# Images innermost in the DRAM buffers of a recurrent scan, fewer and larger transfers, and VectorE instead of TensorE for an addition

## The chip, the cores and the metric

The kernel runs on one core of a Trainium2 chip. The metric is the device time of one execution in microseconds. Its engines here are TensorE (PE, with its weight loads as PEld), VectorE (DVE), ScalarE (ACT), GpSimd (POOL) and SyncE (SP), which only issues DMA transfers; a queue of an engine is written SPq or ACTq.

## The reference

x has 4 images, 512 channels and 64 x 64 pixels, so 4096 tokens an image, all in float32. Four layers follow each other, each of the form x + layer(group norm of x). Layers 1 and 3 are Fourier mixers, layer 2 a gate; they are not touched. Layer 0 is a recurrent layer over the tokens with 8 heads of 64 and chunks of 16 tokens:

```python
def step(carry, inp):
    W1c, b1c = carry
    xq, xk, xv, et = inp
    Z1 = xk @ W1c + b1c
    grad = _ln_l2_bwd(Z1, xv - xk, g, bb)
    Attn1 = jnp.tril(xq @ xk.swapaxes(-1, -2))
    b1_bar = b1c - jnp.tril(et) @ grad
    Z1_bar = xq @ W1c - et * Attn1 @ grad + b1_bar
    last_eta = et[..., -1, :, None]
    W1n = W1c - (last_eta * xk).swapaxes(-1, -2) @ grad
    b1n = b1c - (last_eta * grad).sum(-2, keepdims=True)
    return ((W1n, b1n), xq + _ln(Z1_bar, g, bb, EPS_IN))
...
return _ln(out, post_w, post_b, EPS_IN) @ o_w.T
```

The result, with the bias that `post_b` gives and with x added, is x1, the input of layer 1.

## The kernel before

Layer 0 has two parts. `project` makes, for every block of 512 tokens of an image, keys, targets and rates (a record of 196 numbers a token and head, tensor `records` in DRAM) and the rotated queries (`queries`). ScalarE issues both stores (L1203, L1205), one pair for each 128 tokens. At its end ScalarE writes rows of zeros behind the records of every image, which the scan's loads ahead of need may touch (L1234, 8 transfers).

`scan_and_read` then runs 256 steps of 16 tokens, over all 4 images and 8 heads at once, in two groups of two images (g = 0 and 1). The partitions are 4 head pairs x 16 tokens x 2 heads of a pair. A step of a group goes: TensorE makes Z from the state and the keys (`project_k`, L2107 and L2113), ScalarE sums its squares (`spread`, L1798), VectorE makes the gradient from it (`gradients`, L1963 to L1989), GpSimd the sum of gradients and the scaled gradient (`stored`), TensorE adds to the state in PSUM (`update`, L2125) and ScalarE copies the state out (`state_out`, L1791). The state of the next step needs this one, so each group is a chain.

Beside the chain runs the reading of 128 tokens of one image, a tile. There are 32 blocks (`sc`) of 128 tokens (eight steps) and 4 images, so 128 tiles, one for every two steps; two steps with one tile are called a slot here. A tile is worked on with a lag: `KQ`, `OUT`, `NORM`, `PROJ`, `LEAVE` = 4 to 8 slots behind the scan. The even or the odd step of a slot (`at.odd`) has its fixed part of it. `project` of the tile is L2195: 4 x 4 products with the output weights, and for each of the 4 channel blocks one product of the identity with the image (L2198), which adds x in PSUM. `leave` (ScalarE, L1845) adds the bias while it copies out; `moments` (VectorE, L1997) takes the statistics for the next layer.

All engines run a program written out by hand: eight steps twice in the body of a loop (`Fori(1, SC // 2)`), the first and last turns outside it. Instructions of an engine run in that order, so a wait holds all behind it. SyncE issues every transfer of the scan from one queue, and waits in it for what a transfer needs:

```python
for g in range(GR):
    sp.wait_ge(state_ps[g].sem, state_ps[g].at(s, -1))
    load_record(g, (c + 2) % RING, s + 2)      # two transfers
...
for g in range(GR):
    sp.wait_ge(stored_sb[g].sem, stored_sb[g].at(s, 1))
    # two stores into gradients
```

Then in an even step the tile's gradients and sums are loaded (`grad_sb`, `b_sb`), in an odd one the query of the next tile, once GpSimd has read the one before (`qb_sb`), and the keys of a later block (`k_in`, which TensorE turns, L2095). y is stored and x loaded a tile at a time in odd steps. `queries` are turned by TensorE in L2176, the result of a tile in L2159.

## Time and profile before

| | |
|---|---|
| median of 3 runs (lowest, highest) | 6241.13 us (6234.36, 6241.5) |
| profiled execution, its own time | 6242.9 us |
| its span, first to last instruction | 6241.0 us |
| busy over the span: PE, VectorE, ScalarE, GpSimd | 86%, 63%, 38%, 38% |
| projection, about | 215 to 1645 us |
| scan, about | 1719 to 4340 us |
| Fourier layers and gate | the rest |
| DMA packets | 823279, of them 357224 under 512 bytes |

Busy time is the time in which an engine has an instruction running; the rest is waiting. An engine's share is a mean over parts with different limits, so it is read for each part. A line such as L2113 is that line of the kernel. "issue" as the cause of a wait means that nothing in the profile shows what the engine waited for.

### The profile page before, as it was taken

Reading aid. Unit: us, or ns where it says so; the run is one execution under the profiler, and the core shown is the slowest. Engines: PE = TensorE matmul, PEld = TensorE weight load, DVE = VectorE, ACT = ScalarE, POOL = GpSimd, SP = SyncE. Lnnn points to the kernel's source line nnn. Section 1 sums busy time; section 2 is a strip of 40 time slices with the busy share of each in tenths; the row PEclk is TensorE's granted clock in tenths of the full one; section 3 lists DMA queues with packets and bytes.
Section 4 is the critical chain, followed back from the end, with each engine's and each line's share of the span. In section 5 each row is a group of like instructions: output and inputs, shape, how many; then the busy total and the mean of one; then the engine's idle time right before and its main releaser. Section 6 shows DMA issues by size and latency. Waiting matters only on the chain. (4 is left out here: it accounts for less than half of the span.)

```text
span 6241.0 us, 144090 instructions
## 1 busy us (share of the span) xinstructions
PE 5393.6 (86%) x42556; PEld 3821.0 (61%) x42556; DVE 3919.7 (63%) x14026; ACT 2368.3 (38%) x6675; POOL 2385.5 (38%) x3910
## 2 busy tenths in 40 slices
PE   1799999999588888888888888888799999599999
PEld 0344444444267777777777777777666666377777
DVE  5566666666377777777767777777566666544444
ACT  0111111111055555555555555555333333233333
POOL 0244444444255455555545554454122222122222
PEclk9899999999779899989999998999899999799999
DMA  6233333333344444444444444444212221222221
GB/s 246 72 128 120 127 120 127 120 128 120 127 106 119 125 119 123 118 122 118 119 119 121 120 120 120 118 122 126 98 77 87 87 87 45 78 88 87 87 87 70
DMA packets 823279, 693.73 MB, mean 111 GB/s; under 512 B 357224, under 2 KB 758000, under 8 KB 811664
## 3 DMA queue, kind: packets, MB, share of 16 engines
q1 hardware_dynamic: 732304, 542.54, 29.1%
q10 hardware_dynamic: 90240, 142.75, 6.1%
q8 instruction: 294, 4.82, 0.3%
q14 instruction: 441, 3.61, 0.2%
HBM read 402.96 MB, written 282.20 MB: 110 GB/s over the span
## 5 line engine op out<-in xcount | busy, mean ns | idle before, releaser
L1390 PE MATMUL proj_ps<-proj_w_sb,proj_h 128*128 128x512 f32 x3072 | 1345.6, 596 | 0.0
L1390 PEld LDWEIGHTS proj_ps<-proj_w_sb,proj_h 128*128 128x128 f32 x3072 | 577.2, 190 | 743.4 <-issue 716.6
L2195 PE MATMUL scan_ps_y<-scan_o_t,proj_wo_sb 128*128 128x128 f32 x4096 | 648.2, 307 | 2.1 <-ACT scan_o_t L1827 2.1
L1312 DVE SCALAR_TENSOR_TENSOR proj_lin<-proj_ps,proj_rstd,proj_wbias_sb 128x512 f32<-128x512 f32 x384 | 284.5, 748 | 545.8 <-PE proj_ps L1390 544.8
L2195 PEld LDWEIGHTS scan_ps_y<-scan_o_t,proj_wo_sb 128*128 128x128 f32 x4096 | 565.1, 214 | 50.8 <-issue 8.6
L1737 POOL TENSOR_TENSOR scan_b_step<-scan_core,scan_rate_last 128x128 f32<-128x128 f32 x512 | 318.6, 622 | 650.5 <-DVE scan_core L1984 650.5
L1963 DVE TENSOR_TENSOR scan_zg<-scan_ps_z,scan_gain 128x128 f32<-128x128 f32 x512 | 146.1, 285 | 563.1 <-ACT scan_square L1798 518.0
L1798 ACT ACTIVATE scan_square<-scan_ps_z 128x64 f32<-128x64 f32 x1024 | 218.6, 220 | 651.0 <-PE scan_ps_z L2113 645.4
L1791 ACT COPY scan_state_w<-scan_ps_w 128x512 f32<-128x512 f32 x480 | 281.3, 586 | 476.1 <-PE scan_ps_w L2125 455.5
L2125 PE MATMUL scan_ps_w<-scan_step,scan_record 64*128 64x128 f32 x4088 | 386.5, 312 | 12.4 <-DVE scan_step L1989 11.9
L1266 POOL TENSOR_TENSOR proj_gk<-proj_rec,proj_gain_sb 128x256 f32<-128x256 f32 x256 | 181.5, 729 | 554.5 <-DVE proj_rec L1333 554.5
L1260 POOL TENSOR_TENSOR proj_by_cos<-proj_lin,proj_rope 128x512 f32<-128x512 f32 x256 | 340.7, 1341 | 137.5 <-DVE proj_lin L1312 108.0
L266 POOL TENSOR_TENSOR fourier_spec<-fourier_prod 128x448 f32<-128x448 f32 (+1 forms) x80 | 86.7, 1084 | 696.3 <-DVE fourier_prod L410 696.3
L281 ACT COPY fourier_turned<-fourier_psT 128x512 f32<-128x512 f32 (+3 forms) x289 | 156.7, 550 | 476.0 <-PE fourier_psT L480 476.0
L2125 PEld LDWEIGHTS scan_ps_w<-scan_step,scan_record 64*128 64x128 f32 x4088 | 301.7, 208 | 49.8 <-DVE scan_step L1989 18.2
L1729 POOL TENSOR_TENSOR scan_rate<-scan_rstd,scan_record 128x2 f32<-128x2 f32 x512 | 102.8, 201 | 598.0 <-DVE scan_rstd L1966 593.2
L1744 POOL TENSOR_TENSOR scan_b_sum<-scan_b_step,scan_b_sum 128x128 f32<-128x128 f32 x512 | 309.6, 605 | 44.9 <-POOL scan_b_step L1737 7.1
L706 POOL TENSOR_TENSOR fourier_spec<-fourier_prod 128x448 f32<-128x448 f32 (+1 forms) x80 | 86.5, 1082 | 619.8 <-DVE fourier_prod L799 619.8
L487 PEld LDWEIGHTS fourier_psD<-fourier_mats,fourier_turned 128*128 128x128 f32 x2148 | 270.4, 192 | 78.8 <-ACT fourier_turned L281 35.2
L487 PE MATMUL fourier_psD<-fourier_mats,fourier_turned 128*128 128x128 f32 x2148 | 288.5, 277 | 34.4 <-DVE fourier_spec L389 31.8
L2113 PE MATMUL scan_ps_z<-scan_state_w,scan_k_t 128*32 128x64 f32 x7680 | 207.2, 228 | 108.0 <-ACT scan_state_w L1791 107.2
L831 PEld LDWEIGHTS fourier_psD<-fourier_mats,fourier_turned 128*128 128x128 f32 x2080 | 260.5, 191 | 43.7 <-issue 22.3
(290 smaller groups left out, 12327.7 us busy)
## 6 DMA issues: line engine op xcount, KB each, us to landing
scan_record<-records SPq DMA_DIRECT2D x1032, 98.0 KB
records<-proj_rec ACTq DMA_DIRECT2D x128, 784.0 KB, 3.6
scan_k_in<-records SPq DMA_DIRECT2D x266, 128.0 KB
spectra<-fourier_spec SPq DMA_DIRECT2D x16, 2112.0 KB, 6.4
fourier_spec<-spectra SPq DMA_DIRECT2D x16, 2112.0 KB, 8.2
stats_x<-x SPq DMA_DIRECT2D x16, 2048.0 KB, 7.7
proj_h<-x SPq DMA_DIRECT2D x32, 1024.0 KB, 7.1
queries<-proj_q ACTq DMA_DIRECT2D x128, 256.0 KB, 3.7
```

Of the source, the lines that this page charges most:

```text
L487: done = pe.matmul(psD[t % 2][:, col:col + P], turned[t % 2][:, j * P:(j + 1) * P], mat, start=True, stop=True)
L831: done = pe.matmul(psD[q][:, col:col + P], turned[q][:, j * P:(j + 1) * P], mat, start=n == 0, stop=n == len(terms) - 1)
L1260: g_.tensor_tensor(by_cos[q][:, n].rearrange("p (a e) -> p a e", e=32), lin[q][:, n].rearrange("p (a e) -> p a e", e=32), cos, ALU.mult).t ...
L1312: v.scalar_tensor_tensor(lin[q][:, n], ps[q][n][:], rstd[k][:, j:j + 1], T.wbias[:, n], ALU.mult, ALU.add).then_inc(lin_sb.sem, 1)
L1390: last = pe.matmul(ps[j % 2][n][:], h[k][:, ct, j * P:(j + 1) * P], T.w[:, n, ct], start=ct == 0, stop=ct == CT - 1)
L1737: v.tensor_tensor(b_step[g][:], core[g][:], rate_last[g][:, :, 2:3].broadcast_to([P, PB, HD]), ALU.mult).then_inc(b_step_sb[g].sem, 1)
L1744: v.tensor_tensor(b_sum[g][(c + 1) % RING][:], b_step[g][:], b_sum[g][c % RING][:], ALU.add).then_inc(b_sum_sb[g].sem, 1)
L1791: a.copy(state_of(g, at)[:].rearrange("p r b a e -> p r (b a e)"), ps_w[:, :, g].rearrange("p r b a e -> p r (b a e)")).then_inc(state_sb[ ...
L1798: a.activation(square[:, g, b], ps_z[g][:, b * HD:(b + 1) * HD], ACT.Square, accum_out=ssq[g][:, b:b + 1]).then_inc(ssq_sb[g].sem, 1)
L2113: done = pe.matmul(ps_z[g][32 * a:32 * a + 32, b * HD:(b + 1) * HD], k_t[q][PB * g + b][:, a, CS * at.c:CS * at.c + CS].rearrange("p t n - ...
L2125: done = pe.matmul(ps_w[:, r, g, b].rearrange("p a e -> p (a e)"), record[g][at.ring][rows, b, 0:2 * HD], step[g][rows, b].rearrange("p a ...
L2195: pe.matmul(ps_y[:, n], T.wo[:, ct, n * P:(n + 1) * P], o_t[:, ct], start=ct == 0, stop=False)
```

## The change

The DRAM buffers `records`, `gradients` and `sum_snapshots` get another order of dimensions, with the images inside the tokens. A record load then takes all four images at once; a gradient store takes the two images of a group, a snapshot too. Records are written by two transfers for each 128 tokens, one for each head of the pairs; a tile's gradients are read by two. Queries, x and y move for four tiles at once, with buffers four times as large, two of each. `leave` goes from ScalarE to VectorE and adds bias and image in one instruction of three operands; the identity products go. The rows of zeros are written at the start of the projection. Buffers that only the projection needs are released before the scan.

```diff
-    rec = dram("records", (B, NH // 2, TOK + 2 * P, 2, RW))
+    rec = dram("records", (NH // 2, TOK + 2 * P, 2, B, RW))
-    grad = dram("gradients", (B, NH // 2, TOK, 2, HD))
-    s_snap = dram("sum_snapshots", (TOK // P * B * P, HD))
+    grad = dram("gradients", (NH // 2, TOK, 2, B, HD))
+    s_snap = dram("sum_snapshots", (TOK // P, 2, P, B // 2, HD))
...
-                    act.dma_start(rec[bass.ds(b, 1), :, bass.ds(g * 512 + j * P, P)].rearrange("o a t n e -> (o t) a (n e)"),
-                                  rec_sb[:, j].rearrange("p (a n) e -> p a (n e)", n=2)).then_inc(rec_out[j].sem, 16)
+                    for n in range(2):
+                        act.dma_start(rec[:, bass.ds(g * 512 + j * P, P), n, bass.ds(b, 1)].rearrange("a t o e -> (o t) a e"),
+                                      rec_sb[:, j].rearrange("p (a n) e -> p a n e", n=2)[:, :, n]).then_inc(rec_out[j].sem, 16)
...
             normalise(0, 0, 0)
+
+            act.wait_ge(init.sem, init.at(0, 1))
+            for a in range(NH // 2):
+                for n in range(2):
+                    act.dma_start(rec[a, TOK + n * P:TOK + (n + 1) * P].rearrange("t n b e -> t (n b e)"), zero[:]).then_inc(pad_out.sem, 16)
             rows_out(0)
...
-        x_sb = [sb(f"x_in{q}", [P, CT, P]) for q in range(2)]
-        y_sb = [sb(f"y{q}", [P, CT, P]) for q in range(2)]
+        x_sb = [sb(f"x_in{q}", [P, UNITS, P]) for q in range(2)]
+        y_sb = [sb(f"y{q}", [P, UNITS, P]) for q in range(2)]
...
-            def load_record(g, ring, s):
-                for b in range(PB):
-                    sp.dma_start(record[g][ring][:, b, :], rec[PB * g + b, :, bass.ds(s * CS, CS)].rearrange("a t n e -> a (t n) e")
-                                 ).then_inc(rec_in[g][ring].sem, 16)
+            def load_record(ring, s):
+                sp.dma_start(record[ring][:].rearrange("p b e -> p (b e)"), rec[:, bass.ds(s * CS, CS)].rearrange("a t n b e -> a (t n) (b e)")
+                             ).then_inc(rec_in[ring].sem, 16)
...
-                        load_record(g, (c + 2) % RING, s + 2)
...
+                    load_record((c + 2) % RING, s + 2)
+                if c == 1 and (scan or p == 0) and (not isinstance(v, int) or v * 2 + p):
+
+                    sp.dma_start(x_sb[1 - p][:], x_view[:, :, bass.ds((v * 2 + p - 1) * P, P)]).then_inc(x_loaded[1 - p].sem, 16)
                 if scan:
                     for g in range(GR):
                         sp.wait_ge(stored_sb[g].sem, stored_sb[g].at(s, 1))
-                        for b in range(PB):
-                            sp.dma_start(grad[PB * g + b, :, bass.ds(s * CS, CS)].rearrange("a t n e -> a (t n) e"),
-                                         stored[g][c % 2][:, b, :]).then_inc(grad_gone[g][c % 2].sem, 16)
+                        sp.dma_start(grad[:, bass.ds(s * CS, CS), :, PB * g:PB * g + PB].rearrange("a t n b e -> a (t n) b e"),
+                                     stored[g][c % 2][:]).then_inc(grad_gone[g][c % 2].sem, 16)
+                if c == 7 and (not isinstance(v, int) or v):
+
+                    sp.wait_ge(y_done.sem, y_done.at(v * 8 + p * 4 - 4, 0))
+                    sp.dma_start(o_view[:, :, bass.ds((v * 2 + p - 2) * P, P)], y_sb[p][:]).then_inc(y_gone[p].sem, 16)
...
+                elif scan:
+                    if c == 3:
+
+                        if not isinstance(v, int):
+                            sp.wait_ge(qb_sb.sem, qb_sb.at(v * 8 + p * 4 - 4, 0))
+                        sp.dma_start(q_sb[p][:].rearrange("p b h e -> p b (h e)"), q_in[:, bass.ds((v * 2 + p) * P, P)].rearrange("b n c -> n b c")
+                                     ).then_inc(q_loaded[p].sem, 16)
...
-                for n in range(CT):
-                    done = a.activation(y_sb[q][:, n], ps_y[:, n], ACT.Identity, bias=T.wo_bias[:, n:n + 1])
-                done.then_inc(y_done.sem, 1)
...
+            def leave(tile):
+                t, b, sc, par, half = tile
+                q = b % 2
+                dve.wait_ge(y_ps.sem, y_ps.at(t, 1))
+                dve.wait_ge(x_loaded[par].sem, x_loaded[par].at(half, 16))
+                dve.wait_ge(y_gone[par].sem, y_gone[par].at(half, 0))
+                dve.wait_ge(stats_sb.sem, stats_sb.at(t, 0))
+                for n in range(CT):
+                    done = v.scalar_tensor_tensor(y_sb[par][:, b * CT + n], ps_y[:, n], T.wo_bias[:, n:n + 1], x_sb[par][:, b * CT + n], ALU.add, ALU.add)
+                done.then_inc(y_done.sem, 1)
...
-                elif norm:
-                    head_norms(norm)
+                else:
+                    if norm:
+                        head_norms(norm)
+                    if gone:
+                        leave(gone)
...
-                    pe.matmul(ps_y[:, n], T.wo[:, ct, n * P:(n + 1) * P], o_t[:, ct], start=ct == 0, stop=False)
-                if n == 0:
-                    pe.wait_ge(x_loaded[b % 2].sem, x_loaded[b % 2].at(sc * 2 + b // 2, 16))
-                done = pe.matmul(ps_y[:, n], T.ident[:], x_sb[b % 2][:, n], start=False, stop=True)
+                    done = pe.matmul(ps_y[:, n], T.wo[:, ct, n * P:(n + 1) * P], o_t[:, ct], start=ct == 0, stop=ct == CT - 1)
```

## Rows read from the trace of the kernel before

**Rows 1.** Order in time of PE: start us, length us, what [wait before it <- releaser].
```profile
1718.62 0.66 PE L2113 MATMUL scan_ps_z<-scan_state_snap,scan_k_t 128*32 128x64 f32 x16 [1.35 <-ACT scan_state_snap L1791]
...
2703.18 0.65 PE L2159 MATMUL scan_ps_turn<-proj_ident_sb,scan_on 128*128 128x128 f32 x4 [0.38 <-ACT scan_on L1821]
...
2720.35 0.65 PE L2159 MATMUL scan_ps_turn<-proj_ident_sb,scan_on 128*128 128x128 f32 x4 [0.37 <-ACT scan_on L1821]
...
2727.65 0.66 PE L2176 MATMUL scan_ps_turn<-proj_ident_sb,scan_q_in 128*128 128x128 f32 x4 [2.17 <-DMA scan_q_in<-queries]
...
4334.98 0.41 PE L2113 MATMUL scan_ps_z<-scan_state_w,scan_k_t 128*32 128x64 f32 x16
```

**Rows 2.** Groups by line, 2500 to 3000 us: count | busy us, mean ns | idle before.
```profile
L1971 DVE SCALAR_TENSOR_TENSOR scan_t_row<-scan_zg,scan_rstd,scan_record 128x64 f32<-128x64 f32 x194 | 46.1, 278 | 0.0
...
L2198 PE MATMUL scan_ps_y<-scan_x_in,proj_ident_sb 128*128 128x128 f32 x192 | 40.0, 293 | 0.0
```

**Rows 3.** Busy us by window: length, PE, PEld, DVE, ACT, POOL, clock, DMA, GB/s.
```profile
2500.00:3000.00 500.00, 425.33 (x5597) 372.12 (x5595) 362.21 (x1830) 281.74 (x974) 255.88 (x530) 0.91 0.45 120
```

**Rows 4.** Waits, 2500 to 3000 us: total us, times, longest us.
```profile
DVE scan_zg L1963 <- ACT scan_square L1798: 95.4, 44, 7.0
...
PE scan_ps_turn L2176 <- DMA scan_q_in<-queries: 37.8, 18, 4.8
...
DVE scan_zg L1963 <- issue: 12.6, 3, 4.9
```

**Rows 5.** Order in time of SyncE's queue, one slot: start us, length us.
```profile
2720.29 4.10 SPq L1677 DMA_DIRECT2D gradients<-scan_stored  x4
2724.64 0.48 SPq L1633 DMA_DIRECT2D scan_q_in<-queries  x1
...
2726.97 2.94 SPq L1623 DMA_DIRECT2D scan_record<-records  x4
2730.11 2.96 SPq L1677 DMA_DIRECT2D gradients<-scan_stored  x4
...
2738.32 0.42 SPq L1667 DMA_DIRECT2D x<-scan_y  x1
```

**Rows 6.** DMA queues in 2729:2733, 2733.5:2734.5, 2735:2736, 1650:1664: packets, MB, share of 16.
```profile
q1 hardware_dynamic: 435, 0.33, 26.2%
...
q1 hardware_dynamic: 282, 0.07, 31.7%
...
q1 hardware_dynamic: 623, 0.27, 97.5%
...
q10 hardware_dynamic: 3424, 5.19, 104.1%
```

**Rows 7.** Order in time of VectorE, parts of three slots.
```profile
2679.68 0.29 DVE L1963 TENSOR_TENSOR scan_zg<-scan_ps_z,scan_gain 128x128 f32<-128x128 f32 x1 [4.93 <-issue]
...
2700.93 0.28 DVE L1963 TENSOR_TENSOR scan_zg<-scan_ps_z,scan_gain 128x128 f32<-128x128 f32 x1
...
2708.92 0.29 DVE L1963 TENSOR_TENSOR scan_zg<-scan_ps_z,scan_gain 128x128 f32<-128x128 f32 x1 [0.79 <-ACT scan_square L1798]
...
2718.46 0.28 DVE L1963 TENSOR_TENSOR scan_zg<-scan_ps_z,scan_gain 128x128 f32<-128x128 f32 x1
```

**Rows 8.** The page's groups by line, the projection's additions.
```profile
L1312 DVE SCALAR_TENSOR_TENSOR proj_lin<-proj_ps,proj_rstd,proj_wbias_sb 128x512 f32<-128x512 f32 x384 | 284.5, 748 | 545.8 <-PE proj_ps L1390 544.8
```

**Rows 9.** Order in time between projection and scan.
```profile
1645.50 11.70 ACTq L1234 DMA_DIRECT2D records<-proj_zero  x8
...
1671.80 0.34 SPq L1615 DMA_DIRECT2D scan_gain<-gain_rows  x1
```

**Rows 10.** Busy by window, columns as in rows 3.
```profile
1646.00:1666.00 20.00, 0.00 (x0) 0.00 (x0) 0.00 (x0) 0.00 (x0) 0.00 (x0) 0.50 1.02 364
1666.00:1672.00 6.00, 0.00 (x0) 0.00 (x0) 0.00 (x0) 0.00 (x0) 0.00 (x0) 0.50 0.00 1
```

**Rows 11.** The page's DMA issues: count, KB each, median us to landing.
```profile
queries<-proj_q ACTq DMA_DIRECT2D x128, 256.0 KB, 3.7
```

More of the change, by code:

```diff
@@ L1432, in each @@
             return [sb(f"{n}{g}", shape) for g in range(GR)]
-        record = many("record", [P, PB, RW], RING)
+        record = [sb(f"record{q}", [P, B, RW]) for q in range(RING)]
         stored = many("stored", [P, PB, HD], 2)
@@ L1541, in scan_and_read @@
         q_loaded = [one(f"q_loaded{q}", 16) for q in range(2)]
-        grad_in = [one(f"grad_loaded{q}", 48) for q in range(2)]
+        grad_in = [one(f"grad_loaded{q}", 64) for q in range(2)]
         x_loaded = [one(f"x_loaded{q}", 16) for q in range(2)]
@@ L1750, in gained @@
             def gained(tile):
-                t, b, sc, _ = tile
+                t, b, sc, par, half = tile
                 pool.wait_ge(zo_sb.sem, zo_sb.at(t, 2))
@@ L1817, in normed @@
             def normed(tile):
-                t, b, sc, _ = tile
+                t, b, sc, par, half = tile
                 act.wait_ge(oshift_sb.sem, oshift_sb.at(t, 1))
@@ L1823, in outputs_turned @@
             def outputs_turned(tile):
-                t, b, sc, _ = tile
+                t, b, sc, par, half = tile
                 act.wait_ge(turn_o.sem, turn_o.at(t, 1))
@@ L1829, in outputs_out @@
             def outputs_out(tile):
-                t, b, sc, _ = tile
+                t, b, sc, par, half = tile
                 act.wait_ge(zgain_sb.sem, zgain_sb.at(t, 0))
@@ L1854, in query_turned @@
             def query_turned(tile):
-                t, b, sc, _ = tile
+                t, b, sc, par, half = tile
                 act.wait_ge(turn_q.sem, turn_q.at(t, 1))
@@ L1860, in head_roots @@
             def head_roots(tile):
-                t, b, sc, _ = tile
+                t, b, sc, par, half = tile
                 act.wait_ge(hsq_sb.sem, hsq_sb.at(t, 1))
@@ L1866, in output_squares @@
             def output_squares(tile):
-                t, b, sc, _ = tile
+                t, b, sc, par, half = tile
                 act.wait_ge(o_done.sem, o_done.at(t, 1))
@@ L1872, in output_root @@
             def output_root(tile):
-                t, b, sc, _ = tile
+                t, b, sc, par, half = tile
                 act.wait_ge(ovar_sb.sem, ovar_sb.at(t, 2))
@@ L1878, in body @@
             def body(at, scan):
-                kq, out, norm, proj, gone = (at.tile(n) for n in (KQ, OUT, NORM, PROJ, LEAVE))
+                kq, out, norm, proj = (at.tile(n) for n in (KQ, OUT, NORM, PROJ))
                 following = Place(at.v, at.p, at.c + 1) if at.c < 7 else Place(at.v + at.p, 1 - at.p, 0)
@@ L2011, in head_sums @@
             def head_sums(tile):
-                t, b, sc, _ = tile
+                t, b, sc, par, half = tile
                 dve.wait_ge(zsq_sb.sem, zsq_sb.at(t, 1))
@@ L2017, in variance @@
             def variance(tile):
-                t, b, sc, _ = tile
+                t, b, sc, par, half = tile
                 dve.wait_ge(nmean_sb.sem, nmean_sb.at(t, 1))
@@ L2026, in shift_of @@
             def shift_of(tile):
-                t, b, sc, _ = tile
+                t, b, sc, par, half = tile
                 dve.wait_ge(ostd_sb.sem, ostd_sb.at(t, 1))
@@ L2034, in head_norms @@
             def head_norms(tile):
-                t, b, sc, _ = tile
+                t, b, sc, par, half = tile
                 dve.wait_ge(hstd_sb.sem, hstd_sb.at(t, 1))
@@ L2044, in weights @@
             def weights(tile):
-                t, b, sc, _ = tile
+                t, b, sc, par, half = tile
                 dve.wait_ge(kq_ps.sem, kq_ps.at(t, 1))
@@ L2146, in tile_weighted @@
             def tile_weighted(tile):
-                t, b, sc, par = tile
+                t, b, sc, par, half = tile
                 for n in range(2):
@@ L2154, in tile_outputs_turn @@
             def tile_outputs_turn(tile):
-                t, b, sc, par = tile
+                t, b, sc, par, half = tile
                 pe.wait_ge(on_sb.sem, on_sb.at(t, 1))
@@ L2189, in tile_project @@
             def tile_project(tile, n):
-                t, b, sc, par = tile
+                t, b, sc, par, half = tile
                 if n == 0:
```

160 lines of the change are left out of this document (63 added, 97 removed).

## Prediction

> **What bounds the kernel now.** I read the page first, for the stages, then windows of each stage, and in the scan the waits, SyncE's queue, the DMA packets and VectorE's order in time. The projection before it runs with PE busy all the time, and the Fourier layers behind it are not touched, so the change must earn its time in the scan, from the first product of L2113 at 1718.6 us to the last at 4335.0 [rows 1] and some 5 us of its own tail: 2621 us for 256 steps, or 128 slots of two steps and one tile, 20.5 us a slot. In a stretch of 500 us with 24 slots (192 records of the identity product, eight a slot [rows 2]), PE is busy 85% at a mean granted clock of 0.91, VectorE 72% [rows 3]. Neither is full, yet two runs of L2159, one a slot, can stand 17.2 us apart [rows 1]: that is what the engines need when nothing is late. What is late is the query tile: PE waits for it in 18 of 24 slots, 37.8 us in total [rows 4], for instance 2.17 us at 2727.65 [rows 1], and with PE stand ScalarE's squares and VectorE, which waits 95.4 us for them [rows 4].
>
> Why is it late? SyncE's queue shows the sum [rows 5]: per slot eight record loads (2.94 us for four, twice), eight gradient stores (4.10 and 2.96 us for four), and some eight more of 0.4 to 0.5 us each. That is 5.9 + 7.1 + 3.6 = 16.6 us, and with the gaps between them about 18.5: the queue issues back to back. The query load stands behind four stores in it, and may only be issued when the tile before is read (one buffer per parity).
>
> Under the queue lies a second limit. While only record packets of 784 bytes move, 435 packets take 26.2% of 16 engines for 4 us [rows 6], about four engines: 435 / 4 = 109 per engine, 36.8 ns each. The stores of 256 bytes show 31.7%, with two packets of an engine overlapping; on four engines they take 4 / 282 us = 14.2 ns each. Where 512-byte packets of other transfers move, the share is 97.5%, so those use all 16, 16 / 623 us = 25.7 ns each. The Trainium skill has a rule for this (DMA: Bandwidth & Descriptors, "Why a DMA increments its semaphore by 16 and not by 1"): the slowest dimension of both sides decides how many engines take part. The trace agrees, for both kinds of transfer have the four head pairs outermost on the DRAM side. The four engines' need per slot: records 8 x 32 packets x 36.8 ns = 9.4 us; stores 8 x 32 x 14.2 = 3.6; 1536 packets of 512 bytes over 16, 2.5; keys and sums 1.0; queries 0.7. Sum 17.2 us of 20.5.
>
> **The change, part by part.**
> *SyncE's queue.* Per slot remain 2 record loads, 4 stores, 2 gradient, 2 sum and 2 key loads, and per four slots 2 snapshots and one x, y and query transfer. At 0.74 us for each of the first six (4.10 / 4 = 1.03 for stores at worst) and 0.5 for 7.25 others: 4.4 + 3.6 = 8.0 us, 9.2 at worst. It is no longer a limit. Transfers of 1 MB have no row from this queue; their issue costs between the 0.4 us of a quarter of the size and four times that, 1.6 us, with 11 us of free queue per slot over them.
> *Queries, x, y.* The query for four tiles is issued at step 3 of eight and first read six steps later, two buffers deep. The stall of 37.8 / 24 = 1.6 us a slot goes, and with it PE's slow clock behind it. x is loaded seven steps ahead; y is stored at step 7 with nine steps until its buffer is wanted. Price zero, covered by these steps; without cover a 1 MB transfer of 512-byte packets takes 128 x 25.7 ns = 3.3 us.
> *Records.* One load of 128 x 3136 bytes in place of four. The DRAM side keeps the form of the packets that moved on four engines in the row (four head pairs outermost), so I count four again: 32 packets each. A packet of 1568 bytes takes 16 x 1.041 x 14 us / 3424 = 68 ns [rows 6], 23 bytes per ns, against 21 for 784. At the better rate 136 ns, 4.4 us per step in place of 4.7; at the worse 147 ns, no gain. I take 4.4.
> *Stores and gradient loads.* Half the stores, 512 bytes if batch and head elements merge, the same bytes on the same four engines: 3.6 us a slot at 14.2 ns per 256 bytes (3.3 at 25.7 per 512). The gradient load is two of 512 x 256 bytes: 64 x 14.2 = 0.9 in place of 0.8. The four engines' need becomes 8.7 + 3.6 + 1.7 + 0.9 + 1.0 + 0.7 = 16.6 us a slot.
> *PE.* Four identity products a slot go, eight records, 40.0 / 24 = 1.67 us busy [rows 2], of which part overlaps the neighbours; 1.2 to 1.7 us off a need of at most 17.2 leaves about 15.9.
> *VectorE.* It gets the four additions (`leave`), after `head_norms` and before the second gradient of the even step. In the stretch it waits 95.4 + 12.6 us [rows 4], so its own need, with gaps from write to read, is (500 - 108) / 24 = 16.3 us a slot. The fast slot agrees: from 2700.93 to 2718.46 are 17.53 us with one wait of 0.79 [rows 7], 16.7 at most. The new instruction has the form of L1312 at 128 columns. L1312 takes 748 ns for 512 columns [rows 8] and L1971 278 for 64 [rows 2], by a straight line 345 ns for 128; as they overlap, I take 0.27 us from start to start. Both ends: 4 x 0.22 = 0.9 and 4 x 0.34 = 1.4; I take 1.1 with the wait. VectorE's need becomes 17.4 us, the largest of the four (queue 8 to 9, four DMA engines 16.6, PE 15.9). The 0.79 us that VectorE waited for PE in the fast slot is filled by the additions, so it is not added.
> *ScalarE* loses four activations; it waits 0.6 us for PE and more in a slot, so this is nothing.
> *Turns of the loop.* Every eighth slot has a stall of VectorE that no engine releases: 3 in the stretch, 12.6 us [rows 4], one of 4.93 [rows 7]. It stays, 16 x 4 = 64 us.
> *Remainder.* Slots after a turn run PE at the slow clock, the snapshot adds a copy, and large transfers hit the records now and then. No row prices these together; between 0 and 1 us a slot, I take 0.3, 38 us.
> Scan after: 128 x 17.4 + 64 + 38 = 2329 us, 292 less.
> *The zero rows* of the records are written at the start of the projection. Now their eight DMAs begin at 1645.50 behind the last product, and the scan's first transfer is issued at 1671.80 [rows 9]. The DMA engines are idle from 1666, 6 us before that [rows 10]. The last store before them, issued just ahead of 1645.5, lands in 3.7 us [rows 11], at 1649; with the same 6 us the scan begins at 1655: 17 us saved. At the start of the projection 6.4 MB at the rate of now, 5.19 MB in 14 us [rows 6], take 17 us beside the first products; ScalarE issues them where `rows_out(0)` waits for GpSimd anyway. If the queue pushes back as it does now (11.70 us for eight [rows 9]), PE starts up to 6 us late. With a quarter of the packets I take 0. Two stores for one per row block: 0.4 us of an idle ScalarE.
> *Tail.* The last y is 1 MB, 2 to 3 us more; the last tiles lose PE work of 1.2 us each: -3 together.
> Sum: -292 - 17 - 3 = -312 us from the profiled execution's 6242.9 us, which gives 5931; the median of the runs is 1.8 us lower, so 5930.
>
> **Rivals.**
> A. *VectorE is the new bound*, as above: 5930, with 5870 to 6010 for additions of 0.9 to 1.4 us and a remainder of 0 to 0.7.
> B. *The four DMA engines stay the bound.* For it: 16.6 us against 17.4 is close, records may gain nothing, and before the change a need of 17.2 came with 20.5, because bursts meet. The 1 MB transfers make bursts larger. Against: no record was ever waited for, and loads run two steps ahead. If half of the present surplus of 3.3 us stays on 17.4, a slot takes 19.0: 128 x 19.0 + 64 = 2496, -125 - 20: 6098. By the rule of the Trainium skill (DMA: Bandwidth & Descriptors, "Why a DMA increments its semaphore by 16 and not by 1") merging transfers doesn't cure the four engines, since the outermost dimension is still four; the 4.4 us a step taken above counts with that.
> C. *More than I count.* If the turn of the loop and the remainder shrink with the DMA waits (fewer instructions to fetch), 128 x 17.2 + 20: -400 and -20: 5820.
> D. *Slower: PE's clock.* VectorE as the bound leaves PE idle 1.5 to 2.5 us a slot in pieces. If the granted clock sits at its lower level (1.2 GHz) instead of 2.4 for much of the slot, PE's 15.9 us grow to 15.9 x (1 + f); the slot passes 20.5 at f = 0.3, and with f = 0.6 is 25.4: +630 us, 6850. For it: the mean is 0.91 even now [rows 3]. Against: the fast slot had gaps of under 1 us and kept the clock; what lowered it were stalls of 2 us and more, and these go.
> E. *No change:* the queue was a symptom and the second gradient's chain holds the slot. The 17.2 us slots speak against it. 6241.
>
> **How the numbers follow.** A 0.62, B 0.20, C 0.10, D 0.05, E 0.03. The likeliest gives 5930. The range runs from between A and C, 5850, to B, 6110, and leaves out most of C, the far end of B, D and E. Under 0.2% (12 us) a measurement of this kernel tells nothing. Faster 0.92, same 0.03, slower 0.05.
>
> **What would show it.** SyncE's queue with gaps of 8 us and more a slot; no wait of L2176 for a DMA; slots of L2159 at 17.4 to 18, with VectorE's waits under 2 us a slot; `leave` at 0.25 to 0.34 us each; the scan starting 17 us earlier. It is wrong if record or gradient loads appear in the waits (B), if the granted clock of the scan falls under 0.8 (D), or if VectorE waits for the squares in every slot, a chain that I held to be covered.

## The result, and the profile after

The changed kernel takes 6131.8 us (median of 4 runs, 6119.6 to 6136.6) against 6241.3 for the kernel before beside it: a ratio of 0.9824, 95% interval 0.9807 to 0.9841, 109 us less. The forecast was 5930 us, in a range of 5850 to 6110. The direction is right; about a third of the gain came. The profiled execution took 6136.6 us, with a span of 6134.8.

PE's order in time gives the scan's first and last state product, as in [rows 1]:

```profile
1700.38 0.66 PE L2103 MATMUL scan_ps_z<-scan_state_snap,scan_k_t 128*32 128x64 f32 x16 [1.35 <-ACT scan_state_snap L1780]
...
4234.01 0.41 PE L2103 MATMUL scan_ps_z<-scan_state_w,scan_k_t 128*32 128x64 f32 x16
```

The scan starts 18.2 us earlier, as the 17 us of the zero rows had it (zeros_last below tests the reason). But it still lasts 2533.6 us where it lasted 2616.4, 19.8 us a slot in place of 20.4; the forecast, turns and remainder included, was 2329 / 128 = 18.2. So nearly all that is missing is missing inside the scan. The busy time by window (columns as in [rows 3]) says that no engine filled up:

```profile
2500.00:3000.00 500.00, 426.46 (x5554) 369.19 (x5553) 402.83 (x1988) 266.31 (x897) 264.71 (x546) 0.89 0.50 123
```

VectorE, the announced bound, is busy 81% of the time, PE 85% as before, at a granted clock of 0.89 in place of 0.91. Its additions are there, 100 of them in the 500 us, so 25 slots. One lasts 342 ns; as they overlap, they keep VectorE busy for 28.0 / 25 = 1.1 us a slot, the price forecast:

```profile
L1976 DVE SCALAR_TENSOR_TENSOR scan_y<-scan_ps_y,proj_wo_bias_sb,scan_x_in 128x128 f32<-128x128 f32 x100 | 28.0, 342 | 0.0
```

What ended the idle time is in the waits of the whole scan, 1700 to 4235 us (total, times, longest):

```profile
DVE scan_zg L1939 <- ACT scan_square L1787: 266.2, 121, 16.5
...
PE scan_ps_out L2129 <- DMA scan_b_in<-sum_snapshots: 116.4, 59, 4.8
...
POOL scan_rate L1718 <- DMA scan_record<-records: 60.8, 49, 3.9
...
DVE scan_t_row L1947 <- DMA scan_record<-records: 39.4, 40, 3.5
...
PE scan_ps_turn L2085 <- DMA scan_k_in<-records: 20.0, 18, 2.5
...
POOL scan_stored L1736 <- DMA gradients<-scan_stored: 10.2, 14, 1.3
```

The first row is not new: over its scan (1718 to 4336 us) the kernel before had 514.0 us of this wait. The query's wait [rows 4] is gone, and in its place stand waits for the sums, the records, the keys and the stores. The prediction had named this: "It is wrong if record or gradient loads appear in the waits (B)". And SyncE's queue, which was to have gaps of 8 us and more a slot, is occupied for 17.5 of 19.8 us (waits between the transfers of a row included), with fewer but longer issues (compare [rows 5]):

```profile
2560.69 3.38 SPq L1683 DMA_DIRECT2D scan_b_in<-sum_snapshots  x2
2564.39 0.62 SPq L1624 DMA_DIRECT2D scan_record<-records  x1
2565.20 0.39 SPq L1658 DMA_DIRECT2D scan_x_in<-x  x1
2565.81 8.93 SPq L1662 DMA_DIRECT2D gradients<-scan_stored  x2
2574.99 1.65 SPq L1629 DMA_DIRECT2D scan_k_in<-records  x2
```

The record issue shown is cheap (0.62 us for what took 2.9). Two gradient stores behind a record and a 1 MB image load take 8.93 us to issue, 8.1 of them the first store alone, and two sum loads 3.38. With the records on more engines (rec_by_pair, below) two sum loads are issued in 0.89.

Last, the number of engines. In 2522 to 2523 us only record packets move, 3136 bytes each (packets, MB, share of 16 engines):

```profile
q1 hardware_dynamic: 32, 0.10, 25.8%
```

A quarter of 16 engines, four, 129 ns a packet, 4.1 us a load: a little better than the 136 ns and 4.4 us forecast. By the prediction's own sum, with this rate, the four engines would need some 16 us of a slot. The slot takes 19.8. The sum takes every packet at the length that it has when its kind moves alone, and among other traffic packets are longer: over 1800 to 3900 us a record packet lasted 172 ns on the mean. If an engine carries one at a time, a slot's two loads take 2 x 32 x 0.172 = 11.0 us of the four engines and not 8.3, an estimate from these two figures.

### The profile page after: what moved, and what is told of

Read it like the earlier page. It is cut to its first block and busy times, and to the rows that moved or that the text cites. A ratio compares the mean times of both kernels' runs of the same rounds, so it can differ in the third digit from the quotient of the medians.

```text
span 6134.8 us, 138259 instructions
## 1 busy us (share of the span) xinstructions
PE 5355.8 (87%) x41532; PEld 3773.6 (62%) x41532; DVE 4049.2 (66%) x14538; ACT 2249.2 (37%) x6163; POOL 2386.6 (39%) x3910
## 5 line engine op out<-in xcount | busy, mean ns | idle before, releaser
L2185 PE MATMUL scan_ps_y<-scan_o_t,proj_wo_sb 128*128 128x128 f32 x4096 | 624.4, 300 | 1.6 <-DVE scan_y L1976 0.9
L2185 PEld LDWEIGHTS scan_ps_y<-scan_o_t,proj_wo_sb 128*128 128x128 f32 x4096 | 544.2, 207 | 48.8 <-issue 5.5
L2140 PE MATMUL scan_ps_out<-scan_grad_in,scan_weigh 128*128 128x64 f32 x2048 | 337.2, 334 | 0.0
L2140 PEld LDWEIGHTS scan_ps_out<-scan_grad_in,scan_weigh 128*128 128x128 f32 x2048 | 317.2, 244 | 20.2 <-issue 10.8
L487 PEld LDWEIGHTS fourier_psD<-fourier_mats,fourier_turned 128*128 128x128 f32 x2148 | 271.2, 193 | 81.6 <-issue 38.3
L1947 DVE SCALAR_TENSOR_TENSOR scan_t_row<-scan_zg,scan_rstd,scan_record 128x64 f32<-128x64 f32 x1024 | 272.1, 306 | 39.7 <-DMA scan_record<-records 39.4
```

The lines of the kernel that those rows point to most:

```text
L487: done = pe.matmul(psD[t % 2][:, col:col + P], turned[t % 2][:, j * P:(j + 1) * P], mat, start=True, stop=True)
L1947: v.scalar_tensor_tensor(t_row[g][:, b], zg[g][:, b], rstd[g][:, b:b + 1], record[at.ring][:, PB * g + b, 2 * HD:3 * HD], ALU.mult, ALU.ad ...
L2140: done = pe.matmul(ps_out[n][:, a, 0:HD], weigh[n][:, a], grad_sb[b % 2][:, 2 * a + n], start=False, stop=True, skip_group_check=True)
L2185: done = pe.matmul(ps_y[:, n], T.wo[:, ct, n * P:(n + 1) * P], o_t[:, ct], start=ct == 0, stop=ct == CT - 1)
```

## The experiments

Four theories. *1:* the four DMA engines that carry records and stores remain the bound, and the long issues are its symptom (rival B). *1a:* the 1 MB transfers add to it, by more than their bytes. *2:* VectorE is the bound (the prediction). *3:* SyncE's queue by its number of issues. The expectations of the first runs call 1a theory 2. The kernel before took 6240.5, 6249.5, 6253.7 and 6246.0 us beside the four groups of runs, so kernels are compared by their ratio to it. All intervals are about 0.0016 to either side. Percentages from here on are differences of these ratios, so shares of the time before.

| kernel | edit | median us | ratio to before |
|---|---|---|---|
| after | the change | 6131.8 | 0.9824 |
| rec_by_pair | record load in 4 transfers, by head pair | 5840.7 | 0.9362 |
| rec_by_image | in 4 transfers, by image | 6019.1 | 0.9651 |
| rec_by_group | in 2 transfers, of two images | 6003.0 | 0.9599 |
| rec_padded | 1 transfer, 784-byte pieces | 6174.1 | 0.9877 |
| leave_back | additions back on ScalarE and PE | 6128.6 | 0.9822 |
| rec_by_pair_leave_back | rec_by_pair and leave_back together | 5811.9 | 0.9296 |
| all_by_pair | the same, and the stores by head pair | 5825.4 | 0.9313 |
| all_by_pair_by_tile | all_by_pair, and images, outputs, queries by tile | 5847.3 | 0.9349 |
| by_tile | after, images, outputs, queries by tile | 6068.4 | 0.9709 |
| by_tile_by_group | by_tile and rec_by_group | 5961.0 | 0.9538 |
| by_tile_leave_back | by_tile and leave_back: the layout alone | 6074.4 | 0.9725 |
| x_first | after, image load ahead of the record load | 6066.4 | 0.9711 |
| zeros_last | after, zero rows at the projection's end | 6150.3 | 0.9836 |
| before_queries | before, queries four tiles at a time | 6220.4 | 0.9970 |
| before_rec_by_pair | before, record load by head pair | 5887.4 | 0.9414 |

**Which engines carry the records: rec_by_pair.**

```diff
-sp.dma_start(record[ring][:]..., rec[:, bass.ds(s * CS, CS)].rearrange("a t n b e -> a (t n) (b e)"))
+for a in range(HP):
+    sp.dma_start(record[ring][32 * a:32 * a + 32]..., rec[a, bass.ds(s * CS, CS)].rearrange("t n b e -> (t n) (b e)"))
```

> The changed kernel, with each step's record load issued as four transfers of one head pair each (32 partitions of 3136 B) in place of one transfer whose outermost dimension is the 4 head pairs. Theory 1 (four DMA engines are the bound): in the trace of the changed kernel, stretches with nothing but records under way show 25.8% of the engines' time, four engines of sixteen, and a load alone takes 4 x 32 packets of 0.125 us over 4 engines, 4.0 us a step or 8.0 us of the 19.8 us slot, mixed with other traffic more. Spread over sixteen engines it needs a quarter of that: SyncE's issues of sums, keys and gradients fall from 2.6 to 5.3 us back to 0.9 to 1.4 us, VectorE's waits for the record (39.4 us) and PE's for the sums (117.4 us) go, and a slot falls towards its fast ones, 16.7 us: 64 x 2 x (19.8 - 17.0) = 360 us less at best, so 5770 to 5900 us. Theory 2 (the 1 MB transfers of images, outputs and queries hold up everything behind them): record loads are as late as before, 6100 to 6150 us. Theory 3 (the issuing of SyncE's queue is the bound): six more issues a slot at 0.5 to 0.7 us add 3 to 4 us to a queue that holds 19.8 us already, 6200 us or more.

Measured 0.9362: 4.6% below the changed kernel, as theory 1 had it. Theory 3 is out, since SyncE issues six transfers a slot more. VectorE did not set the slot of the changed kernel either, since its work is the same here and the slot is shorter. Not all of the 4.6% is owed to the engines: four transfers that stay on the four engines give 1.7% (rec_by_image, below), so the engines' own part, at the same number of issues, is 2.9%. Its busy row for 2500 to 3000 us, and its first and last state product:

```profile
2500.00:3000.00 500.00, 443.01 (x6337) 383.70 (x6338) 454.84 (x2262) 304.65 (x1024) 298.23 (x621) 0.98 0.55 142
```

```profile
1703.69 0.55 PE L2104 MATMUL scan_ps_z<-scan_state_snap,scan_k_t 128*32 128x64 f32 x12 [1.35 <-ACT scan_state_snap L1781]
...
3934.68 0.41 PE L2104 MATMUL scan_ps_z<-scan_state_w,scan_k_t 128*32 128x64 f32 x16
```

A slot takes 17.4 us, PE's granted clock is back at 0.98, and in this stretch no compute engine waits for a DMA: VectorE's wait for the squares is 3.1 us where it was 40.5. By the page, a quarter of a record lands 2.2 us after its issue; two sum loads are issued in 0.89 us:

```profile
scan_record<-records SPq DMA_DIRECT2D x1032, 98.0 KB, 2.2
```

```profile
2523.74 0.89 SPq L1684 DMA_DIRECT2D scan_b_in<-sum_snapshots  x2
```

And in 2516.5 to 2517 us, where 33 of 49 packets are records, the DMA engines show

```profile
q1 hardware_dynamic: 49, 0.10, 76.1%
```

twelve engines' worth in place of four, and 33 record packets started in half a microsecond where 32 took a whole one. The rule of the Trainium skill (DMA: Bandwidth & Descriptors, "Why a DMA increments its semaphore by 16 and not by 1"), that the slowest dimensions of the two sides set the number of engines, fits: that dimension was 4 before the edit, with 25.8% of 16 engines in the trace, and is 32 after it, with 76.1%.

**The same on the kernel before: before_rec_by_pair.**

```diff
-for b in range(PB):
-    sp.dma_start(record[g][ring][:, b, :], rec[PB * g + b, :, bass.ds(s * CS, CS)].rearrange("a t n e -> a (t n) e"))
+for a in range(HP):
+    sp.dma_start(record[ring][32 * a:32 * a + 32], rec[:, a, bass.ds(s * CS, CS)].rearrange("b t n e -> (t n) b e"))
```

> The kernel before, its DRAM layout, sums, stores, queries and images as they were, with only the record tile joined to one for all images and loaded by four transfers of one head pair (32 partitions of 4 pieces of 784 B) in place of four of one image (128 pieces, head pairs outermost): as many issues as before. If the four DMA engines bound the kernel before too, they lose half of their load (8.7 of 17.2 us a slot), the query wait (37.8 us of 500) and the holds of SyncE go, and slots fall from 20.5 to 17.5 to 19 us, 5880 to 6050 us, and the change's larger and fewer transfers were not what the kernel lacked. If SyncE's issues bound it (the prediction's first reading: 16.6 to 18.5 us of issues a slot), as many issues leave it at 6180 to 6240 us.

Measured 0.9414, 5887 us, at the low end of what the four engines were to give. With the old layout, 784-byte pieces, as many issues as before and nothing batched, the way in which one load is cut gives 5.9%, over three times what the whole change gives. This is the cleanest of the experiments: pieces and issues are the same in number and size, and what differs is which pieces a transfer holds (and that a load waits for both groups of images). What the whole change adds to it is 0.5% (0.9362 for rec_by_pair). In 2500 to 3000 us PE's granted clock is 0.99, and the query's wait has shrunk from 37.8 to 8.0 us by itself:

```profile
PE scan_ps_turn L2175 <- DMA scan_q_in<-queries: 8.0, 4, 2.5
```

Both limits that the prediction saw in the kernel before (SyncE's queue, the late query) were symptoms of the four engines that it put under them.

**The query's wait alone: before_queries.** The kernel before with `q_sb` for four tiles and one 1 MB load at the fourth step, eight slots ahead.

```diff
-load_query(t, b, sc)
+sp.dma_start(q_sb[at.p][:]..., q_in[:, bass.ds((v * 2 + at.p) * P, P)].rearrange("b n c -> n b c"))
```

> The kernel before, with one part of the change alone: the queries of four tiles are loaded by one transfer of 1 MB, eight slots ahead, in place of one of 256 KB a tile that PE waited for (37.8 us of 500 us, 18 waits). If that wait was a cause of its own, its removal gives 37.8 / 500 x 2561 = 190 us, 6050 us. If it was only where a full set of four DMA engines showed (records and stores need 17.2 us a slot of them), the wait moves to the record, the sums or the stores, and the gain is under 60 us: 6180 to 6240 us.

Measured 0.9970, 19 us of the 190 that the wait's length promises. The wait moved to the sums and the images (2500 to 3000 us):

```profile
PE scan_ps_out L2133 <- DMA scan_b_in<-sum_snapshots: 18.3, 12, 4.8
...
PE scan_ps_y L2192 <- DMA scan_x_in<-x: 5.8, 8, 1.2
```

**VectorE: leave_back and rec_by_pair_leave_back.** `leave` on ScalarE, identity products on PE, the buffers as in the change.

```diff
-v.scalar_tensor_tensor(y_sb[par][:, b * CT + n], ps_y[:, n], T.wo_bias[:, n:n + 1], x_sb[par][:, b * CT + n], ALU.add, ALU.add)
+a.activation(y_sb[par][:, b * CT + n], ps_y[:, n], ACT.Identity, bias=T.wo_bias[:, n:n + 1])
+pe.matmul(ps_y[:, n], T.ident[:], x_sb[par][:, b * CT + n], start=False, stop=True)
```

> The changed kernel with one part undone: the output bias is added by ScalarE and the image by identity products on PE again, the eleven-engine-neutral rest (buffers, images innermost, transfers) stays. If VectorE is the bound, as the prediction had it, its four additions a tile (342 ns each, 1.37 us a tile and slot) come off every slot: 128 x 1.1 to 1.37 = 140 to 175 us less, 5960 to 5990 us. If the DMA queue is the bound (theory 1 or 2), nothing of it is seen beyond what PE's four more products a tile (about 0.3 us) and ScalarE's four activations (between the steps' squares) cost in the slots that are fast: 6110 to 6170 us.

> rec_by_pair with the biases and images back on ScalarE and PE as in the kernel before. With the record loads spread over more engines no wait of the scan is for a DMA any more, and its slots between the turns of the loop last 17.2 to 17.5 us, what the prediction had set as VectorE's need. If VectorE sets them, four additions of 342 ns a tile less make 1.1 to 1.37 us a slot less: 5841 less 140 to 175 = 5665 to 5700 us. If PE with its chain of waits sets them, PE's 4 more products a tile cost about 0.3 us a slot and the activations come between ScalarE's squares: leave_back's undisturbed slots lasted 17.2 us, so nothing is won: 5820 to 5890 us.

Under the DMA bound nothing (0.9822 against 0.9824). Free of it, 0.9296 against 0.9362: taking the additions off VectorE gains 0.66%, 41 us or 0.3 us a slot; the whole scan's slot goes from 17.4 to 17.2 us. That is just under the second answer expected (5820 to 5890 us): moving the additions to VectorE was a small loss.

It does not say that VectorE had slack in rec_by_pair. Its waits there, 1710 to 3930 us, are

```profile
DVE scan_zg L1940 <- ACT scan_square L1788: 36.6, 31, 4.9
DVE scan_zg L1940 <- issue: 13.8, 6, 2.7
```

and 4.2 us more: 0.4 us a slot of 17.4, so that VectorE's own need is 17.0. In rec_by_pair_leave_back they are 136 us, 1.1 us a slot of 17.2, a need of 16.2. The edit thus took some 0.8 us off VectorE's need, and the slot became only 0.2 to 0.3 us shorter. The edit also puts four products a tile on PE again. That PE then sets the slot is not shown by a run of its own; it fits the prediction's 17.2 us as PE's need with these products. The two limits lie so close that work moved from one to the other wins little.

**How the record load is cut on the same four engines: rec_by_image, rec_padded, rec_by_group.**

```diff
 # rec_by_image                     (rec_by_group: for g, two images at a time)
+for b in range(B):
+    sp.dma_start(record[ring][:, b], rec[:, bass.ds(s * CS, CS), :, b].rearrange("a t n e -> a (t n) e"))
 # rec_padded
-record = [sb(f"record{q}", [P, B, RW]) for q in range(RING)]
+record = [sb(f"record{q}", [P, B, RW + 4]) for q in range(RING)]
+sp.dma_start(record[ring][:, :, 0:RW], rec[:, bass.ds(s * CS, CS)].rearrange("a t n b e -> a (t n) b e"))
```

> Control for rec_by_pair: the changed kernel, with the record load also in four transfers, but one for each image (128 pieces of 784 B each, head pairs outermost in every one), so that the number of issues is the same and the engines are the four of before. Theory 1 (four DMA engines): the load costs these four at least as much, since 4 pieces of 784 B at about 0.038 us (the time of such a piece in the kernel before) are 0.15 us against 0.125 us for one of 3136 B; slower than the changed kernel by 0 to 3%, 6130 to 6300 us, and far from rec_by_pair. Theory 2 (1 MB transfers): little change, 6120 to 6180 us. Theory 3 (issuing): the same as rec_by_pair, 6200 us or more, since both issue six more a slot.

> The changed kernel with one thing altered: the record tile has four more columns for each image, so that a record load is still one transfer with the head pairs outermost (four engines), but in pieces of 784 B in place of 3136 B. It asks why rec_by_image (four issues of 784-B pieces, the same four engines) was 113 us faster than the changed kernel (one issue of 3136-B pieces), which no theory expected. Piece size: stretches in which all engines are busy moved 234 GB/s with the large pieces against 265 GB/s with the small ones, so small pieces alone give it back, 6000 to 6040 us. Spacing: four issues of 0.7 us each let other transfers start between them, and one issue of small pieces does not, 6120 to 6150 us.

> Between the changed kernel (one record transfer a step, 0.9824 of before) and rec_by_image (four, 0.9651): two transfers, of two images each, in pieces of 1568 B, all with the head pairs outermost. If the number of issues over which a load is spread decides, it lies between them, 0.970 to 0.978 of before (6055 to 6105 us). If the size of a piece decided, as rec_padded (one transfer, pieces of 784 B, 0.9877) already speaks against, it would lie at the changed kernel or above, 0.982 to 0.988.

rec_by_image was meant as a control. It stays 2.9% from rec_by_pair at the same number of issues, so the engines matter. But it was 1.7% faster than the changed kernel, and no theory had that. rec_padded says that it isn't the size of a piece: small pieces in one transfer are 0.5% slower, outside both answers expected. rec_by_group says that two transfers do better than four, which its expectation had not either. On the four engines, one record transfer in place of four, which the change counts as a gain, was thus a loss. Part of how it loses is to be seen where an image load meets a record load. One microsecond in which packets of both move, in the changed kernel (2570 to 2571 us):

```profile
q1 hardware_dynamic: 239, 0.16, 115.8%
```

in rec_padded (2585 to 2586 us):

```profile
q1 hardware_dynamic: 277, 0.16, 118.6%
```

and in rec_by_image (2541 to 2542 us):

```profile
q1 hardware_dynamic: 443, 0.25, 95.8%
```

All engines count as occupied in the three, but with the records in one transfer they move two thirds of the bytes, and the size of the pieces changes nothing in it. In the first, the 223 image packets of 512 bytes last 65 ns on the mean, in the last 34.

**The 1 MB transfers: by_tile and x_first.** by_tile moves images, outputs and queries by 256 KB a tile as the kernel before did, in the buffers of the change. x_first only exchanges two issues of SyncE:

```diff
+if c == 1: sp.dma_start(x_sb[1 - p][:], x_view[...])
 load_record((c + 2) % RING, s + 2)
-if c == 1: sp.dma_start(x_sb[1 - p][:], x_view[...])
```

> The changed kernel with one part undone: images, outputs and queries are moved tile by tile again (three transfers of 256 KB a slot, each at its own place in SyncE's order, the queries one slot ahead) in place of three of 1 MB every fourth slot. Theory 1a (a 1 MB transfer, most of whose bytes go over all engines, shuts the record and sum loads out of the four busy ones for as long as it lasts, 8 to 12 us from issue to landing, and SyncE's queue with it): a slot's share of that is given back, up to the 1.2 us by which rec_by_image's slots were shorter, 5980 to 6110 us. Theory 1b (the bytes on the four busy engines alone count; they are the same in both): 6110 to 6160 us. The prediction (larger and fewer transfers are what the change wins by): 6150 to 6220 us, with PE's wait for the query back.

> The changed kernel with one order exchanged on SyncE: at the second step of a four-tile group the 1 MB image load is issued ahead of the step's record load, not 0.8 us behind it. In the changed kernel the gradient store issued behind that pair is held 8.8 us on average, in rec_by_image (where the image load comes 3.1 us after the first record issue) 5.0, in rec_by_pair 3.0. If a full record load ahead of the 1 MB transfer is what stretches it (the landing takes 12.4 us there, 8.3 in rec_by_image), the hold falls to 3 to 6 us and each fourth slot is 2 to 5 us shorter: 32 x 2 to 5 = 60 to 160 us less at best, 5990 to 6080 us by the changed kernel's 0.9824 of before. If only the sum of the work on the four engines counts, 6120 to 6150 us.

by_tile: 0.9709, 1.15% or 72 us faster than with the batches, although PE waits for the query again (157.2 us in the scan, 195.2 in the kernel before). x_first: 0.9711, as much from one order of issues, once in eight steps. Its rows:

```profile
2622.03 0.39 SPq L1655 DMA_DIRECT2D scan_x_in<-x  x1
2622.76 1.55 SPq L1624 DMA_DIRECT2D scan_record<-records  x1
2624.53 1.65 SPq L1663 DMA_DIRECT2D gradients<-scan_stored  x2
```

The pair of stores is held 1.65 us, not 8.93; over 1800 to 3900 us the mean is 2.2, not 9.1. From issue to landing (1800 to 3900 us, median) the image load takes

```profile
scan_x_in<-x SPq DMA_DIRECT2D x26, 1024.0 KB, 12.4
```

in the changed kernel, and

```profile
scan_x_in<-x SPq DMA_DIRECT2D x27, 1024.0 KB, 6.6
```

in x_first. So a whole record load standing on four engines ahead of a transfer that needs all sixteen doubles that transfer's time. SyncE's queue as a whole is freed of little: the long hold goes, records and keys are issued more slowly, and its issues add up to 15.1 us a slot where they were 15.4. The Trainium skill (DMA: Bandwidth & Descriptors, "Queues, rings and completion order") says that one issuing engine's transfers are consumed in order on each DMA engine. That fits with a start behind the record load on those four, and so does the end: in 2574 to 2576 us of the changed kernel, with no record packet left, packets of 512 bytes, the image load's and those of the stores behind it, keep only 28.9% of 16 engines occupied, four or five. It does not say why the other twelve slow down as well, as the 65 ns of an image packet show; no run here shows that step.

**Does the split only help against the 1 MB transfers? by_tile_by_group.**

> by_tile (no 1 MB transfers, one record transfer a step, 0.9709 of before) with the record load in two transfers of two images as in rec_by_group. If the gain of two transfers (0.9824 to 0.9599 in the changed kernel) comes from the meeting of a whole record load with a 1 MB transfer, it is not there without these: 0.966 to 0.973. If it is a property of the record load by itself, it is there again: 0.945 to 0.955, and then better than either.

Measured 0.9538 against by_tile's 0.9709: 1.7% of the 2.3% is there without any 1 MB transfer, as the second answer had it (0.945 to 0.955). Most of the gain of two transfers over one belongs to the record load itself. Its cause stays open.

**The parts of the change: by_tile_leave_back and zeros_last.**

> The new DRAM layout (images innermost, fewer record, store and sum transfers, zero rows early) alone: images, outputs and queries tile by tile, biases and images added by ScalarE and PE as before. by_tile is 0.9709 of before; with the additions back on ScalarE and PE, leave_back says no change with the four engines full (0.9822 against 0.9824), rec_by_pair_leave_back 0.7% less without: 0.965 to 0.973. If the layout alone were worth less than the whole change, and batching and VectorE made the rest (the prediction), 0.985 or more.

> The changed kernel with the zero rows of the records written at the end of the projection again, with the eight transfers of the new layout. The prediction gave their move 17 us: the scan's first state product came 18 us earlier in the changed kernel. Mine: 12 to 19 us slower than the changed kernel, 6144 to 6151 us, with the whole difference ahead of the scan's first product. Rival: the start of the scan came earlier by the new layout of the transfers themselves, and the zero rows cost nothing at either place: within 5 us of the changed kernel.

The layout alone (records, stores, sums, zero rows) gives 0.9725. The additions on VectorE make 0.9709 of it, no difference beyond the intervals. The batching makes 0.9824 of that. So the change won 2.8% by one part and gave 1.2% back by another. With the zero rows late, the scan's first state product comes 17.6 us later than in the changed kernel:

```profile
1717.95 0.66 PE L2103 MATMUL scan_ps_z<-scan_state_snap,scan_k_t 128*32 128x64 f32 x16 [1.35 <-ACT scan_state_snap L1780]
```

The ratio, 0.9836 (0.9822 to 0.9850), is 0.12% up; it holds 17.6 us (0.28%) as well as none. The trace decides for the start of the scan: the rival is out. That the run as a whole loses 17 us by it is not shown.

**The stores too: all_by_pair and all_by_pair_by_tile.** The `stored` tiles are joined for all images and leave in four transfers of one head pair, 1024-byte pieces.

```diff
+for a in range(HP):
+    sp.dma_start(grad[a, bass.ds(s * CS, CS)].rearrange("t n b e -> (t n) (b e)"), stored[c % 2][32 * a:32 * a + 32]...)
```

> rec_by_pair_leave_back (5812 us, 0.9296 of before) with the gradient stores also in four transfers of one head pair, for all images at once (32 partitions of 1024 B; four issues a step where there were two). If the four DMA engines still held something up after the records left them (stores had 3.6 us a step of theirs, and SyncE's store issues are held 3.7 to 4.0 us), the holds go and slots lose up to 0.5 us: 5740 to 5800 us. If PE's chain sets the slots (its waits name no DMA any more), nothing: 5800 to 5830 us. If the two more issues a step, or the store waiting for both groups, are late for the gradient load, 5830 to 5900 us.

> all_by_pair with images, outputs and queries tile by tile as in by_tile: the version in which neither a four-engine transfer nor a 1 MB one is left. If the large transfers still cost something (in rec_by_pair they took 5.8 to 6.6 us to land, and the keys loaded behind them 4.7), 10 to 60 us less than all_by_pair. If they cost only with the four engines full, the same as all_by_pair within 15 us. If nine more issues in four slots are one too many for SyncE, 10 to 60 us more.

0.9313 against 0.9296, no gain: with the records away the stores on the four engines hold nothing up. Tile by tile it is 0.9349, 0.36% slower, and 13 of PE's waits are for the query again (19.4 us). So the batches cost only while the four engines are full, and where they are not they gain a little; whether by these waits or by nine issues fewer in four slots is not shown. The fastest version is rec_by_pair_leave_back, 5811.9 us, 7.0% under the kernel before and 5.3% under the changed one.

## Why the prediction was wrong

- **The step that failed** is the overlap that the choice of the bound rests on: "VectorE's need becomes 17.4 us, the largest of the four (queue 8 to 9, four DMA engines 16.6, PE 15.9)". It took the largest of four needs as the slot, and so let four DMA engines meet 16.6 us of need within 17.4 us at no cost. They took 19.8 us a slot for some 16 us of it; with the records on more engines the slot is 17.4 and no DMA is waited for in 2500 to 3000 us. Rival B happened; its slot, 19.0 and the turns of the loop, is 19.5, and its 6098 us are 34 below the measured time. The prediction had the warning in its own words, "before the change a need of 17.2 came with 20.5", and gave B 0.20.
- **"Price zero"** for queries, x and y is the term inside it that was most wrong. It compared the transfers with their due times, and no engine waits for one of them; but their cost falls on others. by_tile puts the price at 72 us, and exchanging one order of issues in x_first gains as much (71 us by the ratios).
- **SyncE's queue**, 8.0 us a slot and "no longer a limit", counted issues at a fixed price each. Over 1800 to 3900 us the issues alone, waits left out, add up to 15.4 us a slot. rec_by_pair has six more a slot and they add up to 9.9: the length of an issue depends on what is under way.
- **Records**, 4.4 us a load on four engines: measured 4.1. Right as a rate, and without use, since one transfer of 3136-byte pieces works worse among others than two of 1568 or four of 784 (2.3% and 1.7%).
- **The query's stall** went as forecast, and was worth 19 us in the kernel before, 0.15 us a slot and not 1.6: it was where the shortage showed.
- **VectorE's additions**, 1.1 us a slot: right as work, 28.0 us in 25 slots. Taking them off is worth nothing while the DMA engines bind, and 0.3 us a slot when they don't, since the products that come back with it load PE.
- **Zero rows**, 17 us: 17.6. Their writes at the projection's start held nobody up. **Clock** (rival D): granted 0.89 in 2500 to 3000 us, 0.98 in rec_by_pair, where the waits for DMAs are gone; the fall to under 0.8 did not come.
- **Turns of the loop**, 64 us: VectorE's stalls without a releaser are 48.6 us in the scan (11 of them), 43.3 (11) before, and 13.8 (6) in rec_by_pair, so they shrink with the DMA waits, as rival C had it. The remainder of 0.3 us a slot and the tail's 3 us can't be told apart from the DMA waits.
- **What was right** is VectorE's own need: 17.4 us forecast, 17.0 in rec_by_pair, where VectorE waits 0.4 us a slot. That the slot there, 17.4 with its turns, is the forecast's number is in part chance: the forecast's slot with turns and remainder was 18.2. Once the four DMA engines are out of the way, VectorE is a limit as the prediction said, with PE just under it.

## What to carry to other kernels

Before counting transfers, look at how many DMA engines each of them runs on: a window in which only one kind moves gives it at once (share of 16 against packets). Here a set of four engines that was some 80% full by such a sum (17.2 of 20.5 us, then 16 of 19.8) was the bound, and the waits, the late tile and the long issues elsewhere were its symptoms. In such a case cut the transfer so that its outer dimension spreads, before making it larger. Where few engines are nearly full, do not issue a large transfer right behind a long one on those engines, and price a batch by what is queued behind it, not by when it is due.

## What the runs showed of the hardware that was not expected

- A DMA issue has no fixed length: two stores took 8.93 us (9.1 on the mean) behind a 392 KB load on four engines and a 1 MB load, and 1.65 us (2.2) with these two exchanged.
- A 1 MB load landed in 12.4 us or 6.6 us by this order alone. Beside a 392 KB record load in one transfer, 0.16 MB moved in a microsecond with all engines occupied, whether in pieces of 3136 or of 784 bytes; beside four loads of 98 KB 0.25 MB.
- On the same four engines a record packet of 3136 bytes lasted 129 ns with only records under way (2522 to 2523 us of the changed kernel), 172 on the mean of the scan, and 254 beside a 1 MB load (2570 to 2571 us).
- On the same four engines, with the same bytes and destination, one load of 392 KB, two of 196 KB and four of 98 KB gave 0.9824, 0.9599 and 0.9651 of the kernel before; small pieces in one load 0.9877. Open.
